# Mixer scan: the product with B made with time on the partitions for 12 of 16 states, and another order of the front

## The reference, cut to what matters

```python
xr, z = jnp.split(jnp.einsum('bld,ed->ble', x, in_proj_w), 2, axis=-1)
xc = silu(conv4(xr) + conv_b)                       # causal, 4 taps per channel
dt, Bc, Cc = jnp.split(jnp.einsum('bld,ed->ble', xc, x_proj_w), [16, 32], axis=-1)
dt = jax.nn.softplus(jnp.einsum('blr,dr->bld', dt, dt_proj_w) + dt_proj_b)
dA = jnp.exp(dt[..., None] * -jnp.exp(A_log))
dBx = dt[..., None] * Bc[:, :, None, :] * xc[..., None]
h = dA_t * h + dBx_t; y = jnp.einsum('bdn,bn->bd', h, C_t)     # for each step t
y = (y + Dp * xc) * silu(z)
```

## Time and profile before

| what | us |
|---|---|
| median of 3 runs (lowest, highest) | 7135.28 (7127.81, 7138.75) |
| the profiled execution, its own time | 7135.68 |
| its span, first to last instruction | 7133.4 |
| mixer, first weight load of x's projection to last scan's start | 3845.9 to 5964.6 |

### The profile page before, as it was taken

How to read it: one execution, slowest core, us unless ns; L and a number is a source line. 1 busy time by engine, 2 the same in 40 slices (tenths; PEclk the granted TensorE clock), 3 DMA queues, 4 the chain that set the end, 5 groups by cost and what they waited for, 6 DMA issues and landing times. The chain is left out here.

```text
span 7133.4 us, 118280 instructions
## 1 busy us (share of the span) xinstructions
PE 5442.6 (76%) x36898; PEld 3381.9 (47%) x36898; DVE 5159.8 (72%) x6459; ACT 3841.4 (54%) x5466; POOL 4031.8 (57%) x2175
## 2 busy tenths in 40 slices
PE   4688888888887888877545667677667676999999
PEld 3466665656665656655432222222222223666665
DVE  1788888888888888788776988988988985121221
ACT  1788888888888888888413344344344342111111
POOL 2777777767777777766322866866866864000000
PEclk7899999999999999999767888888888888999999
DMA  1212121111212121110123443443443443101110
GB/s 37 35 28 39 28 40 28 34 30 26 41 26 42 26 40 27 24 36 16 51 95 107 156 139 119 156 142 122 150 145 125 144 139 132 44 29 44 29 44 9
DMA packets 402205, 486.08 MB, mean 68 GB/s; under 512 B 226464, under 2 KB 304032, under 8 KB 401712
## 3 DMA queue, kind: packets, MB, share of 16 engines
q1 hardware_dynamic: 401712, 479.68, 23.2%
...
## 5 line engine op out<-in xcount | busy, mean ns | idle before, releaser
L1409 PE MATMUL c_ps_y<-c_hc,c_ident 128*128 128x512 f32 x2048 | 1108.4, 690 | 640.6 <-POOL c_hc L1435 313.2
L326 DVE CUSTOM_DVE_ANT_0 srow<-srow,ps_s,cur 128x1024 f32<-128x1024 f32 x1024 | 1304.1, 1274 | 331.8 <-PE ps_s L469 284.4
L1428 POOL TENSOR_TENSOR c_db<-c_conv,c_bs 128x1024 f32<-128x1024 f32 x512 | 1199.3, 2368 | 447.7 <-DVE c_conv L1569 347.7
L398 ACT ACTIVATE srow<-srow,nmax 128x1024 f32<-128x1024 f32 x1024 | 1186.1, 1158 | 272.9 <-DVE nmax L326 255.4
L407 ACT COPY AT<-ps_t 128x512 f32<-128x512 f32 x2048 | 1109.1, 593 | 258.1 <-PE ps_t L480 256.5
L480 PE MATMUL ps_t<-ident,srow 128*128 128x128 f32 x8192 | 1139.1, 284 | 17.6 <-ACT AT L407 16.8
L1463 ACT ACTIVATE c_pd<-c_dt,c_a_neg 128x1024 f32<-128x1024 f32 x512 | 571.6, 1117 | 1075.2 <-DVE c_hc L1595 948.6
L480 PEld LDWEIGHTS ps_t<-ident,srow 128*128 128x128 f32 x8192 | 1003.3, 147 | 278.8 <-ACT AT L407 68.3
L469 PE MATMUL ps_s<-K,Q 96*128 96x512 bf16 x2048 | 646.1, 398 | 600.0 <-DVE nmax L326 506.6
L1409 PEld LDWEIGHTS c_ps_y<-c_hc,c_ident 128*128 128x128 f32 x2048 | 421.9, 217 | 1324.5 <-issue 632.6
L1586 DVE TENSOR_TENSOR_SCAN c_pd<-c_pd,c_db 128x1024 f32<-128x1024 f32 x384 | 877.2, 2284 | 38.4 <-ACT c_pd L1463 35.7
...
## 6 DMA issues: line engine op xcount, KB each, us to landing
c_bs<-bc_rows_d SPq DMA_DIRECT2D x256, 512.0 KB, 4.8
c_cs<-bc_rows_d SPq DMA_DIRECT2D x256, 512.0 KB, 4.0
...
ym_d<-c_conv SPq DMA_DIRECT2D x32, 512.0 KB, 2.9
...
```

The costliest lines, as they stand in the source:

```text
L326: nc.vector.tensor_tensor_reduce(r[:], r[:], ps_s[:], cur[k][:, h:h + 1], BIG, ALU.add, ALU.min, nmax[:, h % NROW:h % NROW + 1]).then_inc( ...
L398: nc.scalar.activation(r[:], r[:], ACT.Exp, scale=-1.0, bias=nmax[:, h % NROW:h % NROW + 1]).then_inc(e_ok, 1)
L1409: last = nc.tensor.matmul(ps_y[:, c, cut], ident[:], hc[(2 * n + c) % RING][:, cut], start=n == 0, stop=n == NS - 1)
L1428: nc.gpsimd.tensor_tensor(db[(2 * n + c) % RING][:], conv[:, 2 * pair + c, :], bs[n % RING][:], ALU.mult).then_inc(db_ok, 1)
```

## The change

A unit's product of dt·x with B is made in another form for the 12 states in `ROWS_T`; states 0, 1, 6 and 11 (`ROWS_N`) keep the old way, and their product with C is VectorE's. For the others:

- once a batch TensorE turns B (`turn_b`) and dt·x (`turn_x`, eight transposes of 128x128 a tile), and ScalarE copies both to SBUF (`b_copy`, `x_copy`), so that time lies on the partitions and B of a state is one column per block of 128 steps;
- for each row ScalarE multiplies eight blocks of 128x256 by that column (`scaled`, four after each decay, one row ahead) into `sT`, a ring of two;
- TensorE transposes them back (`turn_db`), eight for a unit, into `pd[:, c]`, after the scan of the row before has left it;
- the decay goes to an SBUF tile `da[c]`, the scan writes `hs` (now four), and GpSimd does the product with C for all of these units.

`xpad` and the turned dt·x share one tile. The order of the front changes: the first two projections of x of the next batch are issued before the last sums of this one, the old batch's skips and gates of tiles 2, 3 lie between the new one's convolutions, all silu(z) come with the next batch's first table, the z projections come after the dt projections, and the softplus of tiles 2, 3 comes after rows 3 and 5 from a raw copy of the projection. All four tiles are stored at the end of the batch. The loops run over B - 1 batches, the last one is written out behind them.

```diff
...
+ROWS_N = (0, 1, 6, 11)
+ROWS_T = tuple(n for n in range(NS) if n not in ROWS_N)
...
+NBS, NDB, NHS, RING, NSC = 2, 4, 4, 4, 2
...
 hc = [sb(f"c_hc{i}", [P, S]) for i in range(RING)]
...
+    def project_r(b, m):
+        if m == 0:
+            pe.wait_ge(xl_in_s, 16 * b + 16)
         for n in range(NH):
             use = NH * m + n
...
+            if use < 4:
+                pe.wait_ge(h_ok, h_at(b, -1, NS - 1, m))
...
+    def turn_b(b):
+        pe.wait_ge(xa_free, NH * CH * b + NH * CH)
+        for k in range(NT):
+            last = nc.tensor.matmul(pd[:, 0, k * NS:(k + 1) * NS], bc[0:NS, k * P:(k + 1) * P],
+                                    ident[0:NS, 0:NS], start=True, stop=True)
+        last.then_inc(bt_ok, 1)
+    def project_z(b, m):
+        if m == 0:
+            pe.wait_ge(bc_ok, NH * b + NH)
+        elif m == 1:
+            pe.wait_ge(pt_free, 2 * NH * b + NH)
+        else:
+            pe.wait_ge(tx_ok, NH * CH * b + NH * (m - 1))
+        for n in range(NH):
+            in_proj(4 + 2 * (m % 2) + n, CH + m, n).then_inc(z_ok, 1)
+    def turn_x(b, m):
+        pe.wait_ge(dtx_ok, CH * b + m + 1)
+        if m < 2:
+            pe.wait_ge(zc_ok, NH * CH * b + NH * (m + 1))
+        else:
+            pe.wait_ge(y_step, CH * b + m - 1 + CH)
+        for k in range(NT):
+            last = nc.tensor.transpose(ps_y[:, m % 2, k * P:(k + 1) * P], conv[:, m, k * P:(k + 1) * P], ident[:])
+            if k % 4 == 3:
+                last.then_inc(tt_ok, 1)
...
+    def turn_db(b, pair, n, c):
+        pe.wait_ge(sc_ok, b * (PAIRS * NT_) + (pair * NT_ + ROWS_T.index(n) + 1))
+        if n - 1 in ROWS_N:
+            pe.wait_ge(hd_ok, hd_at(b, pair, n - 1, c))
+        else:
+            pe.wait_ge(h_ok, h_at(b, pair, n - 1, c))
+        src = sT[ROWS_T.index(n) % NSC]
+        for k in range(NT):
+            last = nc.tensor.transpose(pd[:, c, k * P:(k + 1) * P], src[:, k, c * P:(c + 1) * P], ident[:])
+        last.then_inc(tc_ok, 1)
...
+    def batch(b, more):
         front(b)
...
+        for pair in range(PAIRS):
             for n in range(NS):
                 for c in range(2):
...
+                    if pair and n == 1 and c == 0:
+                        turn_x(b, 2)
+                        turn_x(b, 3)
+                    if n + 1 in ROWS_T:
+                        turn_db(b, pair, n + 1, c)
+                    if n:
+                        sums(b, pair, n - 1, c)
+                    elif pair:
+                        sums(b, pair - 1, NS - 1, c)
+        for c in range(2):
+            if more:
+                project_r(b + 1, c)
+            sums(b, PAIRS - 1, NS - 1, c)
+    for m in range(2):
+        project_r(0, m)
...
+            alone(pool, cs_in[n % RING], cs_fill(b, pair, n), pool_own)
+        alone(pool, acc_ok, at(b, pair, 2 * n + c - RING, 2 * NS), pool_own)
+        alone(pool, h_ok, h_at(b, pair, n, c), pool_own)
+        nc.gpsimd.tensor_tensor(hc[(2 * n + c) % RING][:], hs[(2 * ROWS_T.index(n) + c) % NHS][:],
+                                cs[n % RING][:], ALU.mult).then_inc(hp_ok, 1)
     with pool.Fori(0, B) as b:
...
+        for i in range(2):
+            for c in range(2):
+                times_b(b, 0, i, c)
+        for pair in range(PAIRS):
+            for n in ROWS_T:
                 for c in range(2):
...
+            if pair == 0:
+                act.wait_ge(btc_ok, b + 1)
+                act.wait_ge(xa_free, NH * CH * b + NH * CH)
+        dst = da[c][:]
+        if n in ROWS_N:
+            dst = pd[:, c, :]
+        if n - 1 in ROWS_N and n in ROWS_N:
+            alone(act, hd_ok, hd_at(b, pair, n - 1, c), act_own)
+        elif n in ROWS_N:
+            alone(act, h_ok, h_at(b, *back(pair, n, 1), c), act_own)
         else:
...
+    def scaled(b, pair, n, part):
+        i = ROWS_T.index(n)
+        if part == 0:
+            act.wait_ge(tc_ok, at(b, pair, 2 * (i - NSC) + 1, 2 * NT_))
+            act.wait_ge(btc_ok, b + 1)
+            act.wait_ge(tx_ok, NH * CH * b + 2 * NH * (pair + 1))
+        for k in range(4 * part, 4 * part + 4):
+            last = nc.scalar.activation(sT[i % NSC][:, k, :], dtxT[:, k, pair * PD:(pair + 1) * PD], ACT.Copy,
+                                        scale=bT[:, k, n:n + 1])
+        if part:
+            last.then_inc(sc_ok, 1)
...
+    def first(b, old):
+        act.preload_act_table_set("silu_and_others")
+        for m in range(CH):
+            if old and m == 0:
+                z_silu(b - 1, 0)
+                z_silu(b - 1, 1)
+            x_part(b, m, old)
+            if m:
+                x_silu(b, m - 1)
+            if old and m and m < 3:
+                z_silu(b - 1, 1 + m)
+        x_silu(b, CH - 1)
...
+    def log_late(b, m):
+        act.wait_ge(xc_ok, CH * b + m + 1)
+        act.wait_ge(rc_ok, NH * (2 * b + m - 1))
+        nc.scalar.activation(dt[:, m, :], conv[:, m, :], ACT.Abs).then_inc(sp_a, NH)
+        soft(b, m)
...
+        for n in range(NH):
+            act.wait_ge(z_ok, NH * (CH * b + m) + n + 1)
+            nc.scalar.copy(sz[:, m, half(n)], bank(4 + 2 * (m % 2) + n)).then_inc(zc_ok, 1)
...
+    def batch(b):
+        bc_copy(b)
         act.preload_act_table_set("natural_log_exp_and_others")
...
+        log_part(b, 0)
+        log_part(b, 1)
+        b_copy(b)
+        decay(b, 0, 0, 0)
+        z_copy(b, 0)
+        decay(b, 0, 0, 1)
+        z_copy(b, 1)
+        x_copy(b, 0)
+        decay(b, 0, 1, 0)
+        x_copy(b, 1)
+        z_copy(b, 2)
+        decay(b, 0, 1, 1)
+        for part in range(2):
+            scaled(b, 0, 2, part)
+        z_copy(b, 3)
         for m in range(2, CH):
...
+            raw_part(b, m)
+        for pair in range(PAIRS):
+            for n in range(0 if pair else 2, NS):
                 for c in range(2):
...
+                    if pair and n == 1 and c == 1:
+                        x_copy(b, 2)
+                        x_copy(b, 3)
+                        scaled(b, pair, 2, 0)
+                        scaled(b, pair, 2, 1)
+                    elif n != 1 and n + 1 in ROWS_T:
+                        scaled(b, pair, n + 1, c)
+                if pair == 0 and n in (3, 5):
+                    log_late(b, 2 + n // 4)
...
+            gated(b - 1, 0)
+            gated(b - 1, 1)
+            dve.wait_ge(sc_ok, PAIRS * NT_ * b)
+        nc.vector.memset(xpad[:, :, 0:TAPS - 1], 0.0).then_inc(pad_ok, 1)
+        dve.wait_ge(pad_ok, b + 1)
+        convolve(b, 0)
+        convolve(b, 1)
+        if old:
+            with_skip(b - 1, 2)
+        convolve(b, 2)
+        if old:
+            with_skip(b - 1, 3)
+        convolve(b, 3)
+        if old:
+            gated(b - 1, 2)
+            gated(b - 1, 3)
...
+        dve.wait_ge(sp_v, 2 * (CH * b + m + 1))
+        nc.vector.scalar_tensor_tensor(dt[:, m, :], conv[:, m, :], 0.0, dt[:, m, :], ALU.max, ALU.add
+                                       ).then_inc(dt_ok, 1)
...
+    def scan(b, pair, n, c):
+        q = 2 * n + c
+        dve.wait_ge(da_ok, b * (CH * NS) + (pair * 2 * NS + q + 1))
+        if n in ROWS_N:
+            j = 2 * ROWS_N.index(n) + c
+            dve.wait_ge(db_ok, at(b, pair, j, 2 * NN))
+            nc.vector.tensor_tensor_scan(pd[:, c, :], pd[:, c, :], db[j % NDB][:], 0.0,
+                                         ALU.mult, ALU.add).then_inc(h_ok, 1)
+        else:
+            j = 2 * ROWS_T.index(n) + c
+            dve.wait_ge(tc_ok, at(b, pair, j, 2 * NT_))
+            dve.wait_ge(hp_ok, at(b, pair, j - NHS, 2 * NT_))
+            nc.vector.tensor_tensor_scan(hs[j % NHS][:], da[c][:], pd[:, c, :], 0.0,
+                                         ALU.mult, ALU.add).then_inc(h_ok, 1)
...
+                if pair == 0 and n in (7, 9):
+                    step_late(b, 2 + n // 8)
+                if pair == 0 and n in (8, 10):
+                    step_x(b, 2 + n // 9)
+                if pair and n == 0:
+                    with_skip(b, 0)
+                    with_skip(b, 1)
...
```

More of the change, by code:

```diff
@@ new lines, in front @@
+            def front(b):
+                for m in range(2, CH):
+                    project_r(b, m)
+                for c in range(CH):
+                    project_x(b, c)
+                project_dt(b, 0)
+                turn_b(b)
+                project_dt(b, 1)
+                project_z(b, 0)
+                project_z(b, 1)
+                turn_x(b, 0)
+                turn_x(b, 1)
+                project_z(b, 2)
+                project_z(b, 3)
+                project_dt(b, 2)
+                project_dt(b, 3)
@@ L1450, in _, with half @@
             nc.scalar.activation(a_neg[:], cols[:, :, TAPS + 3:], ACT.Exp).then_inc(w_ok, 1)
+            def half(n):
+                return slice(n * HALF, (n + 1) * HALF)
             def decay(b, pair, n, c):
-                q = unit(b, pair, n, c)
                 m = 2 * pair + c
@@ new lines, in decay @@
+                dst = da[c][:]
[5 more added lines that the diff above has]
```

(57 more changed lines are left out.)

382 lines of the change are left out of this document (179 added, 203 removed).

## The result

| | us | lowest, highest |
|---|---|---|
| before, median of 4 runs | 7135.4 | 7127.8, 7138.8 |
| changed, median of 4 runs | 6920.5 | 6906.2, 6927.7 |
| ratio, 95% interval | 0.970 | 0.968, 0.972 |
| changed, the profiled execution (span) | 6920.3 (6918.5) | |

A forecast was written before the change was run, and what follows sets the result against it. VectorE was taken to bound the rows, a PE, ScalarE, VectorE chain the front. Front 46.0 plus rows 192.8 gave 238.8 against 265.5 a batch; seven times 26.7, with first-batch gains, made 212.4 less: 6923 us, range 6790 to 7060.

The forecast's parts named there:

- front, with 2.4 for the clock: From a batch's last scan to the next first scan: 43.6 us plus 2.4 for half clock, 46.0 against 51.0.
- stalls, pair 0: rows 0 to 6: Opening rows of pair 0: ScalarE's copies, scalings and late softplus delay VectorE's scans, 9.3 us a batch.
- second skip: Where the pairs meet: GpSimd's owed products with B make VectorE's second skip wait 1.9 us.
- pair 1: rows 2 to 5: Rows 2 to 5 of pair 1, after the late transposes of tiles 2, 3: a stall of 3.2 us.
- clock in the rows: Short stretches of TensorE at half clock in the rows, priced at 2 us a batch.
- rows, with 168.4 of work: All rows of a batch: VectorE work of 168.4 us plus stalls and clock, 192.8 against 214.5.
- first batch and the end together: Outside the seven periods: first batch gains 21.7 us in the rows and 3.8 in its front; the end 0.
- Plain bursts: Three runs of four new-form rows: scans wait for TensorE, with ScalarE in step, 2.5 us each, 7.5 a batch.
- Rival one: In the rows all new work hides behind VectorE: 50.5 us a batch, time about 6733; chance 0.12.
- Two: Rival: ScalarE's scalings in the rows are dearer, 2.04 us a set, 16 a batch, time 7051; chance 0.12.
- Four: Rival: TensorE at 1.2 GHz in the rows; gain gone at 20% of units, about 7210 at 30%; chance 0.09.
- Three: Rival: GpSimd's products contend with each VectorE scan in the rows, 13 us a batch, time 7027; chance 0.07.

The follow-up runs named there:

- e1: Changed kernel with the sums of the second half of each tile's 1024 steps left out on TensorE; median 6851.3 us.
- e2: Changed kernel with two ScalarE scalings of 512 columns instead of four of 256, each scaled by its first block's column; median 6890.7 us.
- e8: Changed kernel with half the sums left out and two wide scalings instead of four narrow ones together; median 6813.1 us.
- e10: Changed kernel with filler matmuls around project_x in the front, their results unread, to keep TensorE from idling; median 6917.9 us.
- e3: Changed kernel without Exp and Ln of the late softplus of tiles 2 and 3; median 6889.9 us.
- e9: Changed kernel with GpSimd's four products with B for pair 1's first two states made before row 12 of pair 0; median 6900.2 us.
- e12: Changed kernel with next projections before the last sums, products with B over rows 10, 13, 15, late softplus after rows 5 and 10; median 6871.6 us.

## Why the prediction was right

| step | forecast us | measured us |
|---|---|---|
| first taps, last tap's end after E | 7.4, 26.8 | 7.5, 26.8 |
| softplus 0 starts, softplus 1 ends | 32.0, 40.1 | 33.5, 40.2 |
| front, with 2.4 for the clock | 46.0 | 44.5 |
| stalls, pair 0: rows 0 to 6 | 9.3 | 10.7 |
| rows 7 to 11 | 0.5 | 0.9 |
| burst 12 to 15 | 2.5 | 2.7 |
| second skip | 1.9 | 3.2 |
| pair 1: rows 2 to 5 | 3.2 | 5.1 |
| two bursts | 5.0 | 3.1 |
| clock in the rows | 2.0 | about 3.7 or more, in the stalls above |
| rows, with 168.4 of work | 192.8 | 194.4 |
| period | 238.8 | 238.8 |
| first batch and the end together | 25.5 | 27.8 |

The stalls are stretches of VectorE's timeline less its work in them (pair 0, rows 0 to 6: 42.1 from first scan to row 6, less 4 x 3.45 and 8 x 2.20).

- **The mechanism** was the forecast one: VectorE's rows go from its own pace to that of two chains, and gain about half of what they lose in products with C: 20.1 us a batch for 32 products of 1.25, 40. I had both chains at 2.68 a unit; TensorE's is 2.59, since eight transposes follow in 0.87, not 0.96, and ScalarE's 2.63. e1, e2 and e8 show both by taking them away.
- **The scalings** at 1.59 against my 1.65. The Trainium skill (ScalarE: Activation LUTs, What ACT_TABLE_LOAD costs; the prediction names the section behind it) gave an estimate of 1.60, and this trace agrees with it better than with my value.
- **The front** by its steps came within 0.1 up to the last tap. My 2.4 for the clock was too much: the low clock did come (the last `project_x` 3.58, at full clock 1.92 in e10) and put softplus 0 late by 1.5, but turning B cost less than I had, as its 16 small matmuls run between the dt projections, and by the end of softplus 1 only 0.1 was left. The last dt·x took 2.72, not 2.05, as GpSimd's first product with B had begun before it.
- **Mis-sized stalls.** Two errors nearly cancel. Plain bursts I had too dear, 2.5 each. The wait does begin with the fifth unit, but costs 0.39 a unit, not 0.48, and the 0.5 that I added for ScalarE is not there: 1.5 (pair 1: 3.1 for 5.0). The clock in the rows I had too cheap, 2.0. It costs about 3.7 in three places alone, an estimate from rows: pair 0's burst 20.4 for 19.1; sums ahead of the second skip 2.66 long for 1.88; at row 2 of pair 1 a unit's sums 3.41 for 1.72, start to start. The last two are most of the misses at the skip (3.2 for 1.9) and at the opening of pair 1 (5.1 for 3.2). Then 1.6 too little in the rows stands against 1.5 too much in the front, so that the period agrees to 0.1 is luck: single terms are off by up to 2.
- **The opening of pair 0** is ScalarE's, as forecast, though its first waits are put down to TensorE (3.91 and 2.03 at row 2). From the decay of row 2 (4377.77) to that of row 4 (4391.77) ScalarE pauses once, for 0.21; so row 4 would start about when it does even with row 2 earlier. It comes 31.7 after the first scan, forecast 29.9.
- **The late softplus** held row 4 as forecast (e3: 3.4 a batch).
- **The gates ahead of the taps** took 4.49, not 2.4, beside GpSimd's last product. The taps wait 3.08 more behind them, for ScalarE's copies of TensorE's projections, so it hid.

Rival one fails: no burst runs at 2.20 to its end unless work is taken from both chains. Two fails: scalings are 0.40 apart. Four fails: eight transposes take 0.87 and the windows of steady rows grant 0.99 and 1.00, 0.94 over all rows; low stretches come to some 12% of them by that (an estimate), below its 20%. The Trainium skill's rule of no full clock for transposes (TensorE: Matmul & The Clock Gate, Part 4) is not what these rows show. But the transposes stand between sums here; whether transposes alone would run at full clock, no run shows. Three fails for scans: GpSimd's products beside them take 2.37. Beside VectorE operations on two SBUF tiles they do slow down, to 3.34 in e9 and e12 and 3.33 in the changed kernel. First e9, then the changed kernel, a step size and the product beside it:

```profile
4419.90 3.34 POOL L1513 TENSOR_TENSOR c_db<-c_conv,c_bs 128x1024 f32<-128x1024 f32 x1
...
4426.50 1.31 DVE L1762 SCALAR_TENSOR_TENSOR c_dt<-c_conv,c_dt 128x1024 f32<-128x1024 f32 x1
4426.69 3.33 POOL L1510 TENSOR_TENSOR c_db<-c_conv,c_bs 128x1024 f32<-128x1024 f32 x1
```

The Trainium skill (GPSIMD Engine Reference, Specifications) says the same of such inputs, and the trace agrees.
